# Two operand transposes of a decoder layer done by transposing transfers instead of TensorE, and work moved across the iteration's border

## The reference

```python
z = softmax(einsum('bse,he->bsh', x, W_A) * SCALING, axis=1)          # 16 heads
roll = zp[:, :, (i - j) % S] * (j <= i)                               # zp is z transposed
v = einsum('bse,fe->bsf', x, W_V).reshape(B, S, H, D)
out = einsum('bhij,bjhd->bihd', roll, v).reshape(B, S, E) @ W_O.T + b_O
...
out = softmax(Q @ K.T / 16 + causal) @ V                              # cross attention
...
out = shared(x) + sum over the top 2 of 16 experts of weight * (silu(x @ wg) * (x @ wu)) @ wd
x = x + attn(norm(x)); x = x + xattn(norm(x), ctx, ctx); x = x + ffn(norm(x))
```

## Time and profile before

| | us |
|---|---|
| three runs | 642.64, 645.68, 646.45 |
| median | 645.68 |
| the profiled execution | 646.66 |
| its span, first to last instruction | 644.9 |
| TensorE busy | 578.3 |
| VectorE busy | 459.1 |

### The profile page before, as it was taken

One profiled execution on the slowest core, in us unless ns is written; L12 is line 12 of the kernel. 1 busy time (PEld: TensorE's weight loads), 2 busy tenths in 40 slices (PEclk: granted clock), 3 DMA queues, 4 the chain that ended last, 5 costly groups with the idle time before them and its releaser, 6 DMA issues. The chain is left out here.

```text
span 644.9 us, 13750 instructions
## 1 busy us (share of the span) xinstructions
PE 578.3 (90%) x5212; PEld 388.5 (60%) x5212; DVE 459.1 (71%) x1137; ACT 224.2 (35%) x450; POOL 195.1 (30%) x221
## 2 busy tenths in 40 slices
PE   2768697989999999999999999999989979997696
PEld 1446365755686566766685667666855666664354
DVE  4485567676976788777877797779786866687363
ACT  3564343434243333333333333332423322322121
POOL 4314230332422322243324242414242312132122
PEclk9979789999999999999999999999999998999899
DMA  7884924296116901292119411951186105000600
GB/s 246 284 268 149 343 78 183 76 277 211 67 35 150 343 4 66 79 291 93 67 45 277 138 65 37 240 183 65 37 183 212 67 34 134 1 1 34 132 2 34
DMA packets 61249, 84.26 MB, mean 131 GB/s; under 512 B 2832, under 2 KB 46736, under 8 KB 60944
## 3 DMA queue, kind: packets, MB, share of 16 engines
q1 hardware_dynamic: 61200, 83.60, 43.6%
HBM read 71.47 MB, written 12.12 MB: 130 GB/s over the span
## 5 line engine op out<-in xcount | busy, mean ns | idle before, releaser
L536 POOL TENSOR_TENSOR mid<-gated,mid 128x512 f16<-128x512 f32 x80 | 93.4, 1167 | 233.3 <-ACT mid L683 233.3
L683 ACT ACTIVATE mid<-gated 128x512 f16<-128x512 f32 x80 | 50.1, 627 | 125.6 <-DVEq L895 125.6
L140 PE MATMUL wide<-w_d,mid 128*128 128x256 f16 x320 | 87.9, 275 | 3.5 <-POOL mid L536 3.5
L878 DVE SCALAR_TENSOR_TENSOR gated<-gated,score 128x512 f32<-128x512 f32 x80 | 54.3, 679 | 47.3 <-ACT gated L678 47.3
L141 PE MATMUL wide<-w_d,mid 128*128 128x256 f16 x320 | 87.8, 274 | 0.0
L142 PE MATMUL wide<-w_d,mid 128*128 128x256 f16 x320 | 87.8, 274 | 0.0
L140 PE MATMUL score<-h3T,w_gu 128*128 128x512 f16 x160 | 61.3, 383 | 5.0 <-DVEq L120 3.5
L678 ACT ACTIVATE gated<-score 128x512 f32<-128x512 f32 x80 | 47.2, 590 | 47.5 <-PE score L142 42.6
L140 PE MATMUL rows<-h3T,w_gu 128*128 128x512 f16 x160 | 60.9, 381 | 1.2 <-DVEq L120 1.2
L141 PE MATMUL score<-h3T,w_gu 128*128 128x512 f16 x160 | 61.1, 382 | 0.0
L142 PE MATMUL score<-h3T,w_gu 128*128 128x512 f16 x160 | 61.1, 382 | 0.0
(11 more groups left out here) (193 smaller groups left out, 1384.6 us busy)
## 6 DMA issues: line engine op xcount, KB each, us to landing
toep<-z_scratch SPq DMA_DIRECT2D x16, 2048.0 KB, 16.2
stage<-comb_scratch SPq DMA_DIRECT2D x32, 512.0 KB, 8.0
x_in<-in_x SPq DMA_DIRECT2D x8, 512.0 KB, 10.8
out<-x_out SPq DMA_DIRECT2D x8, 512.0 KB, 3.0
qT<-q_scratch SPq DMA_DIRECT2D x7, 512.0 KB, 3.8
vx<-v_scratch SPq DMA_DIRECT2D x7, 512.0 KB, 5.0
q_scratch<-stage SPq DMA_DIRECT2D x6, 512.0 KB, 5.6
v_scratch<-stage SPq DMA_DIRECT2D x6, 512.0 KB, 6.1
```

The costliest lines, as they stand in the source:

```text
L140: pe.matmul(out, stationary[0], moving[0], start=start, stop=False, **kw)
L536: pool.tensor_tensor(mid[:, 1, j % SLOTS], gated[:, j % SLOTS], mid[:, 0, j % SLOTS], ALU.subtract).then_inc(mid_split.sem, 1)
L683: act.activation(mid[:, 0, j % SLOTS], gated[:, j % SLOTS], ACT.Copy).then_inc(mid_hi.sem, 1)
L878: dve.scalar_tensor_tensor(to, to, 1.0, score.bank(f"g{j}")[:], ALU.add, ALU.mult).then_inc(score.taken.sem, 1)
```

## The change

It does five things. (1) In iterations 2 to 8 the mixture is split into fp16 halves first, straight from `wide`, high part by ScalarE and low part by VectorE, for each half of the heads; SP then moves each half (256 KB) with a transposing transfer, SBUF to SBUF, into mixT. (2) The same for norm 1 of the next batch in iterations 2 to 6: normalised in place in x_in, split into `h1p`, moved by one transposing transfer of 512 KB into h1T. Since x is now read in reversed order within a block (a second input `xr`, arranged on the host), the copies are no longer read backwards, and the residual is loaded on its own into `x_bo`, 512 KB a batch. (3) The z product, its softmax and the logits of the next iteration are computed at the end of this one, and the values `v0` stand in front of the Toeplitz product, which waits for each half of `wide` by itself. (4) h2 and h3 are turned block by block, as soon as two of the four blocks are normalised; h3's turn comes before `down` 7. (5) On VectorE, `part_prob` and the normalisation into h3 stand before the second half of the gate, the statistics of the next x at j = 3 and 4, its normalisation at 5, its split at 6; on GpSimd the bias is added at j = 5. SP's loads of x and of the residual stand before those of `toep`.

`z_product`, `logits`, `z_max` and `z_powers` hold the code that stood in the iteration before, under a name. Cut to its core, blank lines left out:

```diff
--- before.py
+++ after.py
...
-        h1 = sb("h1", [P, C, E])
+        h1p = sb("h1p", [P, 2, K2, C, P], F16)
...
-        mix = sb("mix", [P, C, E])
-        mixT = sb("mixT", [P, 2, K2, S], F16)
+        mix = sb("mix", [P, K2, 2, C, P], F16)
+        mixT_by_k = sb("mixT", [P, K2, 2, S], F16)
+        mixT = mixT_by_k[:].rearrange("p k a s -> p a k s")
...
-        y_taken = sig("y_taken", 1, 2)
+        y_taken = sig("y_taken", 2, 4)
...
-            def load_x(b):
-                sp.wait_ge(h_ready[0].sem, h_ready[0].at(b, 0))
-                sp.wait_ge(x_biased.sem, x_biased.at(b, 0))
-                sp.dma_start(x_in[:], x[b].rearrange("(c p) e -> p c e", p=P)).then_inc(x_loaded.sem, 16)
+            def load_x(b, turned_in=None):
+                if turned_in is not None:
+                    sp.wait_ge(turned.ready.sem, turned.is_ready(turned_in, "h1.1"))
+                elif not isinstance(b, int) or b > 0:
+                    sp.wait_ge(h1p_split.sem, h1p_split.at(b - 4, 1))
+                sp.dma_start(x_in[:], xr[b].rearrange("(c p) e -> p c e", p=P)).then_inc(x_loaded.sem, 16)
+            def load_residual(b):
+                if not isinstance(b, int) or b > 0:
+                    sp.wait_ge(rows.taken.sem, rows.is_taken(b, "o2"))
+                sp.dma_start(x_bo[:], x[b].rearrange("(c p) e -> p c e", p=P)).then_inc(xb_loaded.sem, 16)
+            def move_mix(b):
+                for g in range(K2):
+                    hold(sp, mix_split, mix_split.at(b - 1, g + 1))
+                    sp.dma_start(mixT_by_k[:, g].rearrange("p a (c s) -> p (a c) s", s=P),
+                                 mix[:, g].rearrange("p a c e -> p (a c e)"), transpose=True).then_inc(mixT_moved.sem, 16)
+            def move_h1(b):
+                sp.wait_ge(rows.ready.sem, rows.is_ready(b - 1, "v2"))
+                hold(sp, h1p_split, h1p_split.at(b - 3, 1))
+                sp.dma_start(h1T[:].rearrange("p a k (c s) -> p (a k c) s", s=P),
+                             h1p[:].rearrange("p a k c e -> p (a k c e)"), transpose=True).then_inc(h1T_moved.sem, 16)
...
+                if m and d:
+                    move_mix(it - 1)
...
+                if d and n:
+                    load_x(it + 1, 1 if c == 6 else None)
+                if f and d:
+                    load_residual(it)
...
+                if n and d:
+                    move_h1(it + 1)
...
                 pool.wait_ge(bo_loaded, 16)
+                pool.wait_ge(xb_loaded.sem, xb_loaded.at(b, 16))
                 for c in range(C):
-                    last = pool.tensor_tensor(x_bo[:, c], x_in[:, c], b_o[:], ALU.add)
+                    last = pool.tensor_tensor(x_bo[:, c], x_bo[:, c], b_o[:], ALU.add)
...
+                    if f and j == (5 if d else 3):
+                        add_bias(it)
...
+            def part_h1(b):
+                act.wait_ge(h_ready[0].sem, h_ready[0].at(b, 2))
+                if not isinstance(b, int) or b > 3:
+                    act.wait_ge(h1T_moved.sem, h1T_moved.at(b - 4, 16))
+                act.activation(h1p[:, 0].rearrange("p k c e -> p c k e"), x_in[:].rearrange("p c (k e) -> p c k e", k=K2),
+                               ACT.Copy).then_inc(h1p_hi.sem, 1)
...
             def take_mix(b, g):
                 act.wait_ge(mix_ready.sem, mix_ready.at(b, g + 1))
-                act.activation(mix[:, :, P * g:P * g + P].rearrange("p c (h d) -> p h c d", d=D),
-                               wide[:, g].rearrange("p (h c d) -> p h c d", c=C, d=D),
-                               ACT.Copy, scale=X_MIX / (X_Z * X_V)).then_inc(mix_taken.sem, 1)
+                act.activation(mix[:, g, 0].rearrange("p c e -> p (c e)"), wide[:, g], ACT.Copy,
+                               scale=X_MIX / (X_Z * X_V)).then_inc(mix_hi.sem, 1)
...
+                    if d and j < MID - 1:
+                        part_mid(it - 2, j - 1)
...
+                if n and d:
+                    z_powers(it + 1)
+                elif n:
...
+                    if c % 2:
+                        last.then_inc(h_ready[n].sem, 1)
...
+            def part_h1(b):
+                dve.wait_ge(h1p_hi.sem, h1p_hi.at(b - 3, 1))
+                hi, lo = (h1p[:, a].rearrange("p k c e -> p c k e") for a in range(2))
+                dve.tensor_tensor(lo, x_in[:].rearrange("p c (k e) -> p c k e", k=K2), hi,
+                                  ALU.subtract).then_inc(h1p_split.sem, 1)
+            def part_mix(b):
+                for g in range(K2):
+                    dve.wait_ge(mix_hi.sem, mix_hi.at(b - 1, g + 1))
+                    hi, lo = (mix[:, g, a].rearrange("p c e -> p (c e)") for a in range(2))
+                    dve.scalar_tensor_tensor(lo, wide[:, g], X_MIX / (X_Z * X_V), hi, ALU.mult,
+                                             ALU.subtract).then_inc(mix_split.sem, 1)
...
+                if d and m:
+                    part_mix(it - 1)
...
-                        gate(it, it - 2, j)
+                        open_gate(it, it - 2, j)
+                    if m and j == AHEAD + C + 1:
+                        normalise(it - 1, it, 2, x_res, h3)
+                    at = j - AHEAD
+                    if m and at < C:
+                        part_prob(it, it - 1, at)
+                    if d:
+                        pass_gate(it, it - 2, j)
...
-                        if j == 5:
+                        if d and j in (3, 4):
+                            x_statistics(it + 1, range(2 * (j - 3), 2 * (j - 3) + 2))
+                        if first and j == 5:
                             x_statistics(it + 1)
-                        if j == C + AHEAD:
-                            normalise(it + 1, it, 0, x_in, h1)
+                        if j == (5 if d else C + AHEAD):
+                            normalise(it + 1, it, 0, x_in, x_in)
+                        if d and j == 6:
+                            part_h1(it + 1)
...
+                    score.reach(dve, score.taken, it)
+                    z_max(it + 1)
...
+            def turn_halves(it, use, src, made, b):
+                pe.wait_ge(turned.taken.sem, turned.is_free(it, f"{use}.1"))
+                turned.fill(pe, it, f"{use}.0")
+                turned.reached[(id(pe), True)] = turned.order.index(f"{use}.1") + 1
+                for c in range(C):
+                    if c % 2 == 0:
+                        pe.wait_ge(made.sem, made.at(b, c // 2 + 1))
+                    for k in range(K2):
+                        last = pe.transpose(turned.bank(f"{use}.{k}")[:, P * c:P * c + P], src[:, c, P * k:P * k + P],
+                                            ident[:])
+                        if c == C - 1:
+                            last.then_inc(turned.ready.sem, 1)
...
-                    pe.wait_ge(y_taken.sem, y_taken.at(b, -1))
+                pe.wait_ge(y_taken.sem, y_taken.at(b, g - 3))
                 for n in range(H // 2):
                     head = H // 2 * g + n
-                    acc = wide[:, g, C * D * n:C * D * (n + 1)].rearrange("p (c d) -> p c d", c=C)
+                    acc = wide[:, g].rearrange("p (c h d) -> p c h d", c=C, d=D)[:, :, n]
...
+                if d and (not f or c == 6):
+                    logits(it)
+                if f and (not d or c == 6):
                     pe.wait_ge(turned.taken.sem, turned.is_taken(it - 1, "h1.1"))
-                    for k in range(K2):
-                        last = three_passes(pe, score.bank("z")[0:H, :], parts(w_a, k, slice(None)),
-                                            parts(h1T, k, slice(None)), start=(k == 0), stop=(k == K2 - 1))
-                    last.then_inc(score.ready.sem, 1)
+                    z_product(it)
+                if f and d:
+                    project(it, "v0", h1T, w_v)
                 if m:
                     pe.wait_ge(ctx_taken.sem, ctx_taken.at(1 if first else 5 if c == 6 else 6 if c == 7 else B - 1, UNITS))
                     toeplitz(it, it - 1, 0)
                     toeplitz(it, it - 1, 1)
                 if f:
-                    project(it, "v0", h1T, w_v)
-                if m:
-                    pe.wait_ge(mix_taken.sem, mix_taken.at(it - 1, 2))
-                    turn(it, "mix", mix)
-                if f:
+                    project(it, "v2" if d else "v0", h1T, w_v)
...
+                        pe.wait_ge(mixT_moved.sem, mixT_moved.at(it - 2, 32))
...
-                    turn(it, "h2", h2)
+                    turn_halves(it, "h2", h2, h_ready[1], it - 1)
...
+                if d and not m:
+                    down(it - 2, MID - 3)
                 if m:
-                    pe.wait_ge(h_ready[2].sem, h_ready[2].at(it - 1, 1))
-                    turn(it, "h3", h3)
+                    turn_halves(it, "h3", h3, h_ready[2], it - 1)
+                if d and m:
+                    down(it - 2, MID - 3)
+                if n and d:
+                    score.reach(pe, score.ready, it)
```

(47 more changed lines are left out.)

169 lines of the change are left out of this document (85 added, 84 removed).

## The result

The changed kernel takes 647.91 us (median of 19 runs, 643.59 to 649.76), the kernel before 644.52 beside it (19 runs, 642.28 to 649.77): ratio 1.0044, 95% interval 1.0025 to 1.0064. I had forecast 631 us. The profiled execution has a span of 645.7 us.

What follows compares the result with a forecast made beforehand. It took the steady iteration as a TensorE stream with few holes. From 646.66 us, gains of 5.3 + 12.0 + 2.8 + 0.8 = 20.9 and 6.0 given back led to 631.8; median 1.0 lower: 631 us; range 620 to 666.

Steps and rivals of the forecast that it cites:

- the border's first condition: Before down 7: h3 ready when gate/up 9 ends (381.47), its normalisation running some 1.5 to 2 us earlier.
- a sign of being wrong: At the border: the prediction is wrong if h3 or mid 8 is waited for over 1 us.
- Rival C: Late part of the iteration: VectorE holds it, h3 comes 1.5 late and mid 8 too; 640 us, chance 0.15.
- the border's 12 us: Gate/up 9 to first Toeplitz matmul, iterations 2 to 6: 9.34 falls to 6.96 us, 2.4 each, 12.0 in five.
- The mixture: Iterations 2 to 8: transposes of 0.88 us go, 5.3 gained; waits of 1.0 in six give back 6.0.
- The half rate: Mixture's transposing transfers at half plain rate land at T + 5.2, a wait of 0.8 us; 1.0 taken.
- A (no wait): Mixture's transposing transfers at plain rate, so no wait before the output projection: 623 us, chance 0.27.
- B (4.0 us, clock fallen): Mixture's transfer at quarter rate, TensorE stands 4.0 us in six iterations: 662 us, 652 without the clock; chance 0.23.
- done at T + 0.6 and T + 1.5: VectorE's subtractions of the mixture's two halves, 0.65 to 0.69 us each; T is the end of the Toeplitz matmuls.
- h2 in halves: h2's turn: four transposes (0.46 us), not eight, follow the last normalised block; 0.46 x 6 = 2.8 gained.
- The probabilities: probT's split ahead of the second gate product: the 0.27 us wait goes, 0.8 over iterations 4 to 6.
- The start: Iterations 0 and 1, where DMA is full: the added loads cost 0, with -1 and +3 us as ends.

Runs made afterwards that it cites:

- the two edits that put it in time: Changed kernel with GpSimd's bias add at step 2, not 5, and h1's low split on GpSimd, not VectorE: 633.85 us, ratio 0.9831 to the kernel before.
- the kernel with the border alone: Changed kernel with the bias add at step 2, h1's low split on GpSimd and the mixture turned by TensorE again: 637.40 us, ratio 0.9881.

## Why the prediction was wrong, step by step

- **The forecast as a whole.** 631 us was the time of a kernel whose VectorE is in time at the border. With the two edits that put it in time, and every other part of the change as it is, the kernel measures 633.85. What failed is the border's first condition, and not its size. Against the kernel before, the forecast was a ratio of 0.977 (631 / 645.68) and the result 1.0044, 17.5 us apart; these two edits bring back 13.7.
- **h3 "some 1.5 to 2 earlier, to about 381.5", the step that failed.** I let the normalisation of x move at no extra price (1.35 us in its old place, 3.32 in the new), and priced h1's split at 1.3 us (2.05). Together that is 2.7 us too little, more than the whole advance that I had claimed. VectorE begins h3 0.04 us before gate/up 9 ends (447.55 against 447.59), where it began 0.37 before it in the kernel before. h3 came 1.42 us after TensorE was there, over the 1 us that I had named as a sign of being wrong, and h3T 0.68. The premise that covered both errors was the sentence on the bias add, "to step 5, between splits that leave it idle". I asked what the move does to GpSimd, and not what it does to VectorE beside it. My own rows held the warning: the normalisation of h3, four instructions of the same form as those of x, stands in the earlier trace rows with 2.22 us, and I used that figure without asking why it was not 1.35 (GpSimd's split of `mid` lay beside it, from 381.59 to 382.85).
- **Rival C (VectorE holds the late part, 640 us)** was this mechanism, and I gave it 0.15. It kept 3 of the border's 12 us; in truth none was kept. The row I set against it, the statistics moved into gaps, was true and too small. The row for it, 1.6 us idle of 20.8, deserved a sum: the change takes 1.39 us of statistics out of that stretch and puts in 2.05 for h1's split and 1.97 for the longer normalisation, 2.6 us net into 1.6.
- **The mixture.** The transposes went, 0.88 us, and the wait came: 1.34 us in iteration 6 (1.19 in the row above and 0.15 unnamed before it) against 1.0 forecast, and 1.93 in iteration 8 against 2.3. It is not the same in all: the named wait is 0.24 in iteration 2 and 1.19 to 1.58 in iterations 3 to 7. The half rate was the right choice between the ends. Rivals A (no wait) and B (4.0 us, clock fallen) both fall: the granted clock is 1.00 in all of these stretches, the full 2.4 GHz. The Trainium skill's "Advanced Engine Details and Errata", X-Bar Transpose (TRN2), holds transposing transfers to be as fast as regular ones. This trace does not agree: 512 KB land in 5.1 us transposed and in 3.0 plain (h1T, and the output's store). The 1309 ns that the Trainium skill's "VectorE: DVE Perf Modes", The three transpose paths, gives for one block does not multiply: eight blocks land in 3.2 us.
- **What I missed at the mixture.** I had VectorE's subtractions "done at T + 0.6 and T + 1.5", and the last ended so (396.61 + 1.28 = 397.89, with T = 396.38). But I took the end of the combine weights, ahead of both, as given. Only their place held the first half back; ahead of them it was worth 7.5 us.
- **h2 in halves: the number right, by luck.** The stretch from the output projection to the scores fell by 0.45 us, forecast 0.46. But the halves had nothing to do with most of it. VectorE's and GpSimd's timelines of the kernel before, then VectorE's and TensorE's of the changed one:

```profile
342.66 2.63 DVE L809 TENSOR_SCALAR h<-x_res,mean_var,rstd 128x256 f32<-128x256 f32 x4 [0.30 <-POOL rstd L531]
```
```profile
344.37 3.33 POOL L543 TENSOR_TENSOR x_bo<-x_in,b_o 128x256 f32<-128x256 f32 x4
```
```profile
408.87 2.22 DVE L864 TENSOR_SCALAR h<-x_res,mean_var,rstd 128x256 f32<-128x256 f32 x4 [0.30 <-POOL rstd L570]
```
```profile
411.18 1.04 PE L1201 MATMUL turned<-ident,h 128*128 128x128 f32 x8
```

  The bias add used to lie beside the end of h2's normalisation. With it gone to step 5 the normalisation takes 0.41 us less, and all four blocks are done at 411.09, before TensorE comes to the turn at 411.18. From the output projection to the turn it is 9.12 us instead of 9.49, and only 0.08 went behind it. So the move of the add gave time here and took more at step 5. No run turns h2 as a whole in the changed kernel, so that this is all of it is read from the times, not tested.
- **The probabilities: wrong.** The 0.27 us went, and 0.52 came ahead of the last attend, again VectorE: that stretch is 0.37 longer, where 0.13 was to be gained.
- **The border itself: right once VectorE is in time.** 7.24 us without v0 in the kernel with the border alone, forecast 6.96. That h1's transposing transfer is hidden was right too: its issue takes from 442.07 to 445.66, and no wait of z for it is named.
- **v0 in front of Toeplitz** I counted as neutral. It is for the transfer, whose cover I had worked out; on TensorE's own path it opens a wait of 1.07 us once the mixture is turned by TensorE, as the run with the border alone shows.
- **The start.** The first Toeplitz starts at 44.29 us, 3.3 earlier than before; but between profiles of kernels with the same start it lies anywhere from 42.3 to 46.3. All of these are below the 47.6 of the kernel before, of which there is one profile, so an earlier start is likely and its size can't be told.

## What to carry to other kernels

Before moving an instruction to an idle place on one engine, look at what its neighbour does there: between VectorE and GpSimd an overlap of 1.0 us cost VectorE up to 0.86 here, and one of 2.4 us 1.24, and a row that is longer than its like elsewhere (2.22 against 1.35) says so beforehand. Where an engine is over 90% busy ahead of the point that decides, add up what the change puts there at contended prices before counting any gain that needs it in time. A half that is ready early should leave early: a transfer whose issue takes over a microsecond must not wait for its twin behind unrelated work.

## What the runs showed of the hardware

**VectorE stands for GpSimd on work in SBUF.** Four instructions of 128x256 in fp32, SBUF to SBUF, took 1.37 us alone, 2.09 beside one split of GpSimd (1.16), and 3.32 beside that and the add (2.98). A product of two SBUF operands took 0.69 alone and 1.55 when GpSimd's split started 0.16 us before it. An instruction with an operand in PSUM was not slowed: the first row here starts under the add's last 0.67 us (to 437.02, the row above) and takes the 0.67 of its like. VectorE's and GpSimd's timelines of the changed kernel, the second row the split beside the slowed product:

```profile
436.35 0.67 DVE L956 SCALAR_TENSOR_TENSOR gated<-gated,score 128x512 f32<-128x512 f32 x1
```
```profile
451.07 1.16 POOL L575 TENSOR_TENSOR mid<-gated,mid 128x512 f16<-128x512 f32 x1 [2.51 <-ACT mid L727]
```

The slowed product ends at 452.78, 0.55 us after GpSimd's split (452.23). At half speed beside it for 1.0 us it would have had 0.19 of its 0.69 us left by then, so most of it ran after the split and not beside it. The Trainium skill states this in "SBUF — State Buffer", Who interferes with whom: an instruction of VectorE with two SBUF inputs, or in a two-port mode, and one of GpSimd that reads SBUF exclude each other for the whole instruction. For the product with two SBUF operands and the instruction with one in PSUM the rows agree. The normalisation reads one tensor, so by the Trainium skill it would have to run in a two-port mode, which no row here shows; that it is slowed is measured. By that rule, as an estimate, the moved add could have cost up to its own 2.98 us; 1.24 went when it was taken away. Not everything on GpSimd counts: an instruction of 128x4 elements, listed with 1.01 us from 377.38 on, lay beside the four of 1.35 us in the kernel before and cost them nothing.

**A transposing transfer is dear to its queue.** Its issue occupied SP for 1.3 us at 256 KB (two in 2.67) and 3.59 at 512 KB, most plain ones for 0.33 to 0.49, and it landed 3.2 and 5.1 us after its issue began. The number of DMA packets under 512 B rose from 2832 to 28144.
